# GpSimd's power over the two best scores: one of 32 columns behind the last scatter, or seven small ones ahead of and among the scatters

## The reference

```python
x = x + cross_attention_0(layernorm(x), ctx, mask)     # 32 batches of 128 rows of 128
x = x + moe_0(layernorm(x))                            # 8 experts, 2 per row, capacity 1280
x = x + cross_attention_1(layernorm(x), ctx)
x = x + moe_1(layernorm(x))                            # 16 experts, 1 per row

# moe_0, what matters here
probs = softmax(xf @ router_w + router_b)
topk_p, topk_i = top_k(probs, 2)
topk_p = topk_p / topk_p.sum(-1)                       # weights of the two experts
# each row is put into the buffer of each of its two experts, the experts run over
# their buffers, and the two outputs come back, each times its weight
```

## Time and profile before

| | us |
|---|---|
| median of 3 runs | 833.33 (832.67 to 834.03) |
| profiled execution, device time | 833.27 |
| its span in the trace | 831.5 |
| PE busy | 798.1 (96%) |
| DVE busy | 606.1 (73%) |
| ACT busy | 555.5 (67%) |
| POOL busy | 493.1 (59%) |
| POOL's 64 scatters of the first layer (line 931) | 64.1 |

### The profile page before, as it was taken

The page is one execution under the profiler, slowest core; times in us unless marked ns, Lnnn a source line. Parts: engine busy times, 40 slices in busy tenths (PEclk is TensorE's granted clock), DMA queues, the critical chain, the costliest instruction groups (busy, mean ns, idle before and its releaser), DMA issues.

```text
span 831.5 us, 31624 instructions
## 1 busy us (share of the span) xinstructions
PE 798.1 (96%) x11875; PEld 698.3 (84%) x11875; DVE 606.1 (73%) x1741; ACT 555.5 (67%) x1221; POOL 493.1 (59%) x598
## 2 busy tenths in 40 slices
PE   8999998999899979999999999999999999989997
PEld 3666665666799969999999999999999999989997
DVE  7888888867466568987777777777778667645445
ACT  4898887665677767776666666666575755257662
POOL 6323443667345367876566767575766546548871
PEclk9999999999999999999999999999999999999999
DMA  6444665718344323332421111010101002523215
GB/s 156 136 125 132 211 201 157 195 59 311 109 130 141 110 78 117 117 91 85 158 85 56 29 33 38 25 38 25 38 25 34 16 18 88 107 68 81 73 38 203
DMA packets 86373, 81.84 MB, mean 98 GB/s; under 512 B 15489, under 2 KB 73416, under 8 KB 85458
## 3 DMA queue, kind: packets, MB, share of 16 engines
q1 hardware_dynamic: 76818, 64.27, 26.0%
q0 software_dynamic: 7744, 14.91, 6.0%
q10 hardware_dynamic: 1664, 0.64, 0.5%
HBM read 41.86 MB, written 36.16 MB: 94 GB/s over the span
## 4 chain that ended last, share of the span: by engine, by line
PE 82%; DVE 8%; issue 3%; DMA 2%; ACT 2%; POOL 2%; SPq 0%; ACTq 0%; POOLq 0%; DVEq 0%
PE of L1515 8%; PE sf L1469 8%; PE jf L1390 7%; PE sf L1431 4%; PE sf L1757 4%; PE mf L1417 4%; PE sf L1769 4%; PE jf L1399 4%; DVE cmx L2191 3%; PE sf L1399 3%; PE sf L1641 3%; PE sf L1657 3%; PE mf L1641 2%; PE of L1228 2%; PE sf L1181 2%
## 5 line engine op out<-in xcount | busy, mean ns | idle before, releaser
L1012 POOL TENSOR_TENSOR pl<-pT,ph 128x512 bf16<-128x512 f32 x128 | 146.2, 1166 | 100.2 <-DVE ph L2462 94.2
L2468 DVE TENSOR_REDUCE cmxb<-mf 128x8 bf16<-128x1024 f32 x64 | 78.2, 1221 | 40.7 <-PE mf L1496 40.7
L931 POOL DMA_INDIRECT buf<-gu,slots x64 | 64.1, 1001 | 64.1 <-PE of L1317 14.8
L1989 ACT ACTIVATE pT<-sf 128x1024 f32<-128x1024 f32 x64 | 66.7, 1042 | 23.3 <-PE sf L1479 23.3
L2191 DVE TENSOR_REDUCE cmx<-mf 128x8 bf16<-128x1024 f32 x64 | 78.1, 1220 | 5.1 <-PE mf L1209 3.9
L1001 POOL DMA_INDIRECT gb<-eo,slots x64 | 66.2, 1035 | 19.1 <-issue 18.2
L1469 PE MATMUL sf<-qTs,kTs 64*128 64x128 f32 x1024 | 74.4, 285 | 1.0 <-ACT pT L1989 1.0
L1871 ACT ACTIVATE pTf<-sf 128x1024 f32<-128x1024 f32 x64 | 62.6, 1020 | 11.6 <-PE sf L1188 11.1
L1469 PEld LDWEIGHTS sf<-qTs,kTs 64*128 64x128 f32 x1024 | 62.1, 187 | 6.4 <-issue 1.5
L1390 PE MATMUL jf<-late,oT 128*128 128x128 f32 x496 | 62.9, 280 | 0.0
L1121 POOL DMA_INDIRECT results<-rows x47 | 46.9, 997 | 18.7 <-issue 11.3
(11 more groups left out here) (375 smaller groups left out, 2710.7 us busy)
## 6 DMA issues: line engine op xcount, KB each, us to landing
buf<-zero SPq DMA_DIRECT2D x22, 256.0 KB, 3.9
eo<-zero SPq DMA_DIRECT2D x22, 256.0 KB
late<-in_ctxP SPq DMA_DIRECT2D x24, 192.0 KB, 2.9
rows<-buf SPq DMA_DIRECT2D x71, 64.0 KB, 2.0
gu<-in_gu SPq DMA_DIRECT2D x4, 1024.0 KB, 6.3
kept<-kTs SPq DMA_DIRECT2D x6, 512.0 KB, 3.8
kTs<-kept SPq DMA_DIRECT2D x6, 512.0 KB, 4.2
rows<-buf SPq DMA_DIRECT2D x47, 65.0 KB, 1.9
```

The lines of the kernel that those rows point to most:

```text
L931: nc.gpsimd.indirect_dma_start(out=buf0[:, :], out_offset=bass.IndirectOffsetOnAxis(ap=slots0[:, k, b:b + 1], axis=0), in_=xna0[:, b, :], ...
L1012: nc.gpsimd.tensor_tensor(pl[h][:, :, c, :], pT[h][:, :, c, :], ph[h][:, :, c, :], ALU.subtract)\
L1989: nc.scalar.activation(pT[h][:, :, :, :].rearrange("p r c n -> p r (c n)"), S1, ACT.Exp, scale=D1 ** -0.5)\
L2468: nc.vector.reduce_max(cmx1[b % 2][:, :].rearrange("p (r k) -> p r k", r=2)[:, :, 4 * h:4 * h + 4], M1p[:, :, :].rearrange("p r (c k) -> p ...
```

## The change

The one power over 32 columns becomes seven (`NCHANCES` = `NQD` - 1), each with its own wait: six over the four columns of a quad, and a last one over the eight columns of quads 6 and 7. Pieces 0, 1 and 2 stand at step 31 ahead of the wait for its scores, piece 3 between the second and the third of the four scatters of that step, piece 4 behind the four, piece 5 behind the eight scatters of quad 6, and piece 6 behind the eight of quad 7. DVE takes the difference per quad at the end of `make_slots`, eight times in place of once, and `first_weights` waits for a semaphore of its own.

```diff
+                def chances(n):
+
+                    last = NROUNDS if n == NCHANCES - 1 else n + 1
+                    c = slice(QH * n, QH * last)
+                    pool.wait_ge(odds_done, last)
+                    nc.gpsimd.tensor_tensor(v4[:, c], einv[:, 0:1].broadcast_to([P, c.stop - c.start]), v3[:, c], ALU.pow)\
+                        .then_inc(chances_done, 1)
...
+                        if b == NB - 1:
+                            for n in range(3):
+                                chances(n)
                         if plan[b] and b in ENDING:
                             pool.wait_ge(sf_full, 4 * b + 4)
                         elif plan[b] and b < NB:
                             pool.wait_ge(o_full, O_USE["pv", b - 1] + 1)
-                        for item in plan[b]:
+                        for k, item in enumerate(plan[b]):
+                            if (b, k) == (NB - 1, 2):
+                                chances(3)
                             scatter_front(*item)
+                    chances(4)
                     for item in plan["end"][:EARLIER]:
                         scatter_front(*item)
                     rstd_second(NQD - 1)
...
                     for r in range(NQD - 2, NQD):
                         for item in plan["end", r]:
                             scatter_front(*item)
-                    pool.wait_ge(odds_done, 1)
-                    nc.gpsimd.tensor_tensor(v4[:, :], einv[:, 0:1].broadcast_to([P, NB]), v3[:, :], ALU.pow).then_inc(odds_done, 1)
+                        chances(r - 1)
...
                     nc.vector.tensor_scalar(slots0[:, :, c], slotf[:, :, 0:nb], float(ZROW), None, ALU.add)\
                         .then_inc(slots_ready, 1)
+                    tt(v3[:, c], v1[:, c], v2[:, c], ALU.subtract).then_inc(odds_done, 1)
...
                     if step == 0:
-                        dve.wait_ge(odds_done, 2)
+                        dve.wait_ge(chances_done, NCHANCES)
                         link(ts(v3[:, :], v4[:, :], 1.0, None, ALU.add))
...
                 number_cells()
-                tt(v3[:, :], v1[:, :], v2[:, :], ALU.subtract).then_inc(odds_done, 1)
                 low_ahead(3)
```

More of the change, by code:

```diff
@@ L73 @@
 SINGLE = NB - 5
+NCHANCES = NQD - 1
 def scatters():
@@ L553, in build @@
         rt = sem("rt")
-        odds_done = sem("odds_done")
+        odds_done, chances_done = sem("odds_done"), sem("chances_done")
         sel_ready, rank_ready, out_stored = sem("sel_ready"), sem("rank_ready"), sem("out_stored")
```

## The result

The changed kernel took 835.75 us (median of 20 runs), the kernel before 833.43 beside it (20 runs). The ratio is 1.0032, with an interval of 1.0016 to 1.0047: +2.7 us, between +1.3 and +3.9. The forecast was 835.3, slower by 2.0. The profiled execution took 836.65 us.

A forecast was written before the change was run, and what follows sets the result against it. GpSimd's queue up to the last first-layer scatter, then its landing and the first fetch, was taken to bound the changed stretch. 2.8 - 0.4 - 0.9 + 0.4 + 0.1 = 2.0 us on 833.33 gave 835.3; range 833.8 to 836.9.

The forecast's parts named there:

- The price of a piece: In GpSimd's queue, a piece between two first-layer scatters adds 1.0 us (bounds 0.7 and 1.4).
- Pieces 0 to 2: At batch 31 ahead of its wait, 3.3 us of work fits in 3.59 us idle: cost 0.
- Pieces 3 and 4: Ahead of the second root, two pieces at 1.0 less 0.2 absorbed make it 1.8 us late.
- The landing: The last scatter's landing, 3.73 us before, gets shorter by 0 to 1.3; taken as -0.9 us.
- DVE's differences: Eight small differences replace one large, one per round of slots: 0 to 0.5 us, taken as +0.4.
- the long scatter: One of the last eight scatters, 1.68 us beside a two-input DVE operation, may miss it: -0.71 to 0, taken as -0.4.
- The casts: A DVE cast may meet one of the last two scatters and lengthen it: 0 to +0.7 us, taken as +0.1.
- the clock: TensorE's clock behind the wait for the first tile (214 to 215) stays at half as before: cost 0.
- Pieces that cost nothing: Rival: pieces overlap the making of neighbours' descriptors, leaving only DVE's term: +0.2 us, 833.5; chance 0.03.
- The long power: Rival: the 32-column power delays the last landing; without it landing falls to 2.4, pieces free: -1.3, 831.3; chance 0.03.
- Nothing gives back: Rival: long scatter stays, landing stays 3.73, a cast meets a last scatter: +3.6 us, 836.9; chance 0.16.
- Nearly all back: Rival: landing follows SyncE's stores, only 0.7 late, and returns nearly all: +0.9 us, 834.2; chance 0.22.

The follow-up runs named there:

- third run: The changed kernel as it is, measured once more on a chip where the kernel before takes 832.86 us: 833.74 us, ratio 1.0018.
- the sooner queue: Kernel before, without GpSimd's wait for batch 31's scores and with three scatters instead of two between steps and second root: 830.85 us, ratio 0.9978.
- three spare powers: Changed kernel plus three four-column powers into an unread tile, among the last eight scatters: 836.12 us, ratio 1.0040.
- two spare powers: Kernel before plus two four-column powers into an unread tile, at the places of pieces 3 and 4, long power kept: 833.77 us, ratio 1.0015.
- made twice: Changed kernel with pieces 3 and 4 each computed a second time into an unread tile, on a slower chip: 876.78 us, ratio 0.9946.

## Why the prediction was right, and where it was not

The number was right: +2.0 was forecast, +2.7 measured, and +1.5 on another chip. The queue's part of it was understood. The rest is partly luck: two terms were wrong and cancel, the landing had the right size for a wrong reason, and the path behind the late root was missed.

**The price of a piece** was right. A piece starts with the scatter's end, lasts 1.05 to 1.08, and the next scatter follows after 0.19 and lasts 1.04. That is queueing, as the prediction read the Trainium skill, "GPSIMD Engine Reference", section "2.1 Instruction dispatch"; the trace agrees, with a power starting at most 0.02 us behind its scatter's end, but no row shows single cores.

**Pieces 0 to 2** cost nothing: in the change's third run they end at 172.28, and the first scatter starts where it did. **Pieces 3 and 4** cost 1.83 and 1.86 at the root (1.8 forecast), and **the last scatter** started 2.85 and 2.88 later (2.8). **Piece 6** lies behind it.

**The landing** gave 0.83 and 0.87 (0.9 forecast), but not for the reason given. The forecast let SyncE's stores be late by less than the scatter (0.7 to 1.8). The last store of keys is issued at 209.97 in the third run, where it was at 205.81: 4.2 later, more than the scatter's 2.88. Before, its issue came 0.02 behind the last scatter's; in both traces of the change it comes 1.29 behind, and the landing is shorter: the scatter's packets move at 210.5 to 211.5, while the stores fill the engines until 213. With 0.67 behind, in the sooner queue, the landing takes 3.07; with 1.41 ahead, in the run with three spare powers, 2.58. So the size was right by luck.

**The fetch behind the landing** was left out. It takes 1.9 in place of 3.04, while the load of the row numbers takes 1.06 to 1.11 where it was 0.51. From landing to first transposition it is 3.24 us in both traces, where it was 3.90: another 0.66 given back. The load is slower while the stores still run; with three spare powers they are over by then, and it takes 0.51. The fetch of before isn't explained: its 3.04 us begin at 210.34, when the DMA engines had been idle since 209.25 (0.00 at 210 to 211), so stores and scatters were not in its way. In four of the other five traces from such chips the transposition follows the fetch's issue within 1.9 us, and in the fifth the keys hold it.

**Wrong: "I take 0.4" for DVE's differences.** They cost 0.0 in that trace. With the differences in place the first of the 24 scatters starts at 172.91 against 172.90, and DVE's aggregate at 180.48 against 180.47. Of the bounds given, 0 and 0.5, the lower was true there.

**Wrong: "I take -0.4" for the long scatter.** It stayed, at 1.61. In the third run's timeline of DVE, the operation with two inputs starts 0.14 us ahead of it, as in the earlier trace rows:

```profile
204.06 0.90 DVE L2315 TENSOR_TENSOR past<-lg,cellc 1x720 f32<-1x720 f32 x1
```

DVE's work behind the root is late by about what the scatters are, so the meeting is kept. Three spare powers moved the scatters away from it, and none started inside it. The two errors, 0.4 each, cancel by luck. **The casts** (0.1 forecast) met neither of the last two scatters, which last 0.97 each. With three spare powers one met the last scatter: 1.29.

**Wrong: the clock, "at half ... before and would be after".** At 214 to 215 it stands at full in the third run and was at half before; but from 189 to 195 it stands at half, where it was at full:

```profile
189.00:190.00 1.00, 1.00 (x6) 0.50 0.88 348
...
214.00:215.00 1.00, 0.81 (x4) 1.00 0.42 121
```

All four traces from chips of 833 us with a power at the places of pieces 3 and 4 (the first result, the third run, the three and the two spare powers) have the 1.59 us of idle and the half clock behind it; the kernel before and the sooner queue have neither. That the idle time is what brings the clock down is the likeliest reading, and "made twice", with 3.00 us of idle and the half clock, fits it; filling the 1.59 us would test it, and wasn't tried on such a chip. The forecast followed the late root into ACT, TensorE and DVE, and took each as late by 1.8. In fact the slots of quad 7 are late by 5.2 (197.67 against 192.43), and of the 3.5 us of slack about 1 is left: they are made at 197.84, for a scatter at 199.01. In the run with two spare powers 0.86 us pass from slots to scatter (199.17 to 200.03), so without piece 5 that scatter would have gone at 198.70 and not at 198.03, by this estimate. Piece 5 thus covers 0.7 us of a wait that pieces 3 and 4 make, and the two of them cost more than their place in the queue. The keys end 4.7 later and come to within 0.2 us of holding the first tile. So the change spent the slack of two other paths, which the sum doesn't show. The expert stage starts at full clock now. From its first transposition to the last scatter of the second layer it is 506.5 and 506.8 us in the two traces of the change, and 507.2 before; but with two spare powers, also at full clock, it is 507.1, so that the clock gives this back is not shown.

**The sum by the traces** is +2.88 - 0.87 - 0.66 = +1.35 at the first transposition, and -0.4 behind it: +1.0 at the last scatter of the second layer, for the third run. The kernel was measured at +1.5 (0.1 to 2.8). The traces don't carry the +1.0 to the end: from that scatter on the third run takes 109.2 us, before 110.9, so its profiled execution (832.51) is even shorter than that of before (833.27). The difference lies at one product that waits for DVE:

```profile
730.05 0.33 PE L1646 MATMUL of<-ident,rows 128*128 128x128 f32 x1 [1.31 <-DVE rows L2669]
```

```profile
730.81 0.33 PE L1632 MATMUL of<-ident,rows 128*128 128x128 f32 x1 [3.06 <-DVE rows L2654]
```

The first line is of the third run, the second of the kernel before. It isn't the pieces' work: all four traces of that chip take 109.2 to 109.4 from there on, the sooner queue's without any piece too.

The first result, +2.7 (1.3 to 3.9), lies above the +1.0. Its profiled execution has 2.16 more ahead of the first of the 24 scatters, with the clock at half from 136 to 143. A like stretch stands in the sooner queue's trace, which has no piece at all, and none in the third run's; so it isn't peculiar to the change, and whether it made the first median higher stays open. The forecast's +2.0 lies between the two results; the terms that the traces show give 1.0, below it.

**The rivals.** Pieces that cost nothing are ruled out by the queue's rows; the run with two spare powers has both the long power behind the last scatter and its two pieces at full price. The long power isn't what made the landing 3.73: the sooner queue keeps it, right behind the last scatter, and lands in 3.07. A share of 0.2 isn't excluded (3.07 against 2.86 to 2.90 with the short power). "Nothing gives back" fell with the landing. "Nearly all back" wanted the stores late by only 0.7, and they are late by 4.2; still, 1.5 of 2.88 come back by the first transposition, in two places.

**Left open:** what the waits without a releaser are on the chips of 878 to 880 us, and why kernels with pieces between scatters are faster there; why the first fetch took 3.04 before; and whether the idle time alone brings the clock down.

## What to carry to other kernels

Price a small operation in a queue of transfers by its length and its gap, but then follow the work behind the delayed step: here TensorE idled 1.59 us longer and went on at half its clock, and slack of 3 to 5 us in its other products went that way without a trace in the sum. Work that lies under a landing cost nothing and was best left there. A term that comes out at its size can still rest on a wrong reason: look for the events that it names. A change worth one or two us should be looked at on more than one chip, and its traces counted from an event that it can't move.

## What the runs showed of the hardware that was not expected

- A scatter issued just behind a DVE operation with two inputs takes 1.6 to 1.7 us in place of 0.97: the scatter at 199.97 behind 199.90, at 206.33 in the first result, and at 204.20 behind 204.06. The Trainium skill, "SBUF — State Buffer", section "Who interferes with whom", infers that this kind of operation leaves descriptor making alone; the three traces named don't agree with it. In the other three traces no scatter starts in the first 0.7 us of that operation and none that overlaps it is long; one that starts 0.80 us into it (206.41, two spare powers) lasts 0.97. A cast that starts 0.48 us into a scatter goes with 1.29 (211.80, three spare powers).
- The same program takes 833 us in two of the comparisons and 878 to 880 in two others, on other chips. On the slower ones engines wait up to 5.5 us at a time for nothing shown, and a change of 0.3% has the other sign.
- TensorE's idle 1.59 us at the last quad stands in each of four traces with 7 to 10 us at half clock behind it; the half-clock stretches elsewhere (136 to 143, 137 to 140) come and go between executions of nearly the same program.
